# Two spikes buffers in turn, one transposed input, bias rows by TensorE, stages laid anew

## The reference

```
xn = layernorm(x)                        # x: 4 x 4096 x 512
s  = attn(xn);  g = silu(ffn(xn));  return x + s * g

attn: xs = rmsnorm(xn[:, ::2]) * g_norm;  xp, gate = split(xs @ w_in.T + b_in)
      for each of 2048 steps:  h = tanh(h * A + xt[:, :, None] * Bm)    # 4 x 512 x 64
                               y = h @ Cm.sum(0) + Dv * xt
      out = repeat((y * silu(gate)) @ w_out.T + b_out, 2)
ffn:  spikes = sigmoid(xn @ W_enc + b_enc)                              # 1024 wide
      cont = spikes @ W_s2c + b_s2c                                     # 64 wide
      gate = top 2 of softmax(cont @ Wr + br), 8 experts
      eo = sum_e gate_e * (relu(cont @ W1_e + b1_e) @ W2_e + b2_e)
      layernorm(sigmoid(eo @ W_c2s + b_c2s) @ W_dec + b_dec) * ln_g + ln_b
```

## Time and profile before

| | us |
|---|---|
| median of 3 runs (5712.73 to 5716.41) | 5715.25 |
| the profiled execution | 5713.89 |
| its span | 5712.1 |
| PE busy | 5333.2 (93%) |
| DVE busy | 5449.9 (95%) |
| POOL busy | 5221.4 (91%) |
| ACT busy | 4504.0 (79%) |

### The profile page before, as it was taken

How to read it: one execution, slowest core, us unless ns; L and a number is a source line. 1 busy time by engine, 2 the same in 40 slices (tenths; PEclk the granted TensorE clock), 3 DMA queues, 4 the chain that set the end, 5 groups by cost and what they waited for, 6 DMA issues and landing times.

```text
span 5712.1 us, 92986 instructions
## 1 busy us (share of the span) xinstructions
PE 5333.2 (93%) x30820; PEld 2810.7 (49%) x30820; DVE 5449.9 (95%) x9300; ACT 4504.0 (79%) x9558; POOL 5221.4 (91%) x2764
## 2 busy tenths in 40 slices
PE   6999999999999999999999999999999999999998
PEld 3545545545455455454454554544545545445453
DVE  5999999999999999999999999999999999999998
ACT  5778778787787787877877878778778787787786
POOL 4999999999999999999999999999999999999997
PEclk9999999999999999999999999999999999999999
DMA  6454454444544545444445454444444544444443
GB/s 163 115 122 113 118 122 111 122 113 119 121 113 119 123 109 124 113 118 122 114 118 123 109 125 113 119 121 114 119 123 107 125 114 118 122 114 119 122 108 92
DMA packets 158294, 673.71 MB, mean 118 GB/s; under 512 B 45780, under 2 KB 46840, under 8 KB 92280
## 3 DMA queue, kind: packets, MB, share of 16 engines
q1 hardware_dynamic: 157816, 667.76, 48.5%
HBM read 617.26 MB, written 50.33 MB: 117 GB/s over the span
## 4 chain that ended last, share of the span: by engine, by line
PE 75%; ACT 11%; DVE 8%; issue 4%; SPq 1%; DMA 0%; POOLq 0%; POOL 0%; ACTq 0%; DVEq 0%
PE bank L868 15%; PE ps_y L837 12%; PE bank L927 10%; PE bank L856 8%; PE bank L989 8%; PE ps_acc L989 8%; ACT hidden L676 7%; PE ps_acc L944 4%; DVE ps_z L1109 4%; DVE ps_z L1103 2%; PE bank L910 2%; PE ps_acc L955 2%; PE bank L972 1%; PE ps_acc L972 1%; ACT h L563 1%
## 5 line engine op out<-in xcount | busy, mean ns | idle before, releaser
L497 POOL TENSOR_TENSOR u<-xb,bt 128x1024 f32<-128x1024 f32 x2048 | 4822.6, 2361 | 421.3 <-DVE ps_z L1109 358.3
L563 ACT ACTIVATE h<-ps_z 128x512 f32<-128x512 f32 x4096 | 2419.9, 600 | 839.5 <-DVE ps_z L1109 795.1
L1103 DVE TENSOR_TENSOR ps_z<-h,ps_A 128x512 f32<-128x512 f32 x4096 | 2674.9, 691 | 188.0 <-ACT h L563 106.9
L1109 DVE TENSOR_TENSOR ps_z<-ps_z,u 128x512 f32<-128x512 f32 x4096 | 2660.2, 691 | 0.0
L837 PE MATMUL ps_y<-h,c_wide 128*32 128x512 f32 x8192 | 973.1, 598 | 0.0
L868 PE MATMUL bank<-xnT,w_enc 128*128 128x256 f32 x4096 | 911.9, 381 | 2.0 <-ACT wide L629 2.0
L676 ACT ACTIVATE hidden<-bank,bias_cols 128x256 f32<-128x256 f32 x2048 | 808.0, 475 | 128.5 <-PE bank L927 118.3
L868 PEld LDWEIGHTS bank<-xnT,w_enc 128*128 128x128 f32 x4096 | 772.9, 190 | 185.4 <-issue 83.4
L927 PE MATMUL bank<-contT_both,w 64*128 64x256 f32 x4096 | 582.9, 400 | 198.6 <-ACT hidden L676 105.2
L927 PEld LDWEIGHTS bank<-contT_both,w 64*128 64x128 f32 x4096 | 381.9, 186 | 462.4 <-ACT hidden L676 205.0
L944 PE MATMUL ps_acc<-hidden,w 128*64 128x256 f32 x4096 | 540.3, 389 | 28.9 <-DVE wide L1157 24.2
(11 more groups left out here) (122 smaller groups left out, 3751.4 us busy)
## 6 DMA issues: line engine op xcount, KB each, us to landing
xb<-x_proj_scratch SPq DMA_DIRECT2D x2048, 256.0 KB, 4.6
xbuf<-in_L_attn_x SPq DMA_DIRECT2D x256, 128.0 KB
xres<-in_L_attn_x SPq DMA_DIRECT2D x512, 64.0 KB
out<-g SPq DMA_DIRECT2D x256, 128.0 KB
x_proj_scratch<-xp SPq DMA_DIRECT2D x256, 64.0 KB
w_in<-in_L_attn_w_in SPq DMA_DIRECT2D x1, 2048.0 KB, 8.1
w_enc<-in_L_ffn_W_enc SPq DMA_DIRECT2D x1, 2048.0 KB
w_dec<-in_L_ffn_W_dec SPq DMA_DIRECT2D x1, 2048.0 KB
```

The lines of the kernel that those rows point to most:

```text
L497: pool.tensor_tensor(u[:, tau % 2, :, :], xt, bt[:, :, :], ALU.mult).then_inc(u_ready, 1)
L563: act.activation(h[:, tau % RING, f, :], ps_z[:, f, :], ACT.Tanh).then_inc(h_ready, 1)
L1103: dve.tensor_tensor(ps_z[:, f, :], h[:, (tau - 1) % RING, f, :], ps_A[:, f, :], ALU.mult).then_inc(m_done, 1)
L1109: dve.tensor_tensor(ps_z[:, f, :], ps_z[:, f, :], u[:, tau % 2, f, :], ALU.add).then_inc(z_ready, 1)
```

## The change

Four things. `wide` gets two buffers, by the block's parity, and `xnT` has one instead of two. The bias rows b_dec and b_out are no longer copied by ACT: they lie in one tile `bias_three` with ln_b, and PE adds a row by a matmul with a column of the identity, as it already did for ln_b. So `dec_seed` and `out_seed` are gone, and `decode` (twice) and `fin_out` begin with a `bias_row`. And the table of slots is new throughout.

```diff
-        xnT = sb("xnT", [P, 2, KD, 2, P])
+        xnT = sb("xnT", [P, KD, 2, P])
-        wide = sb("wide", [P, KH, T2])
+        wide = sb("wide", [P, 2, KH, T2])
...
-PE_UP = (19.75, 24.6875, 26.5625, 30.8125, 32.4375, 33.1875, 33.625, 35)
-PE_DOWN = (23.5, 26.5625, 29.3125, 32.75, 33.5, 34.625, 35.5625, 36.5)
+PE_UP = (12.75, 14, 16.0625, 18, 18.75, 20.8125, 22.5, 24.5625)
+PE_DOWN = (14.25, 15.1875, 18.4375, 18.5625, 22.4375, 24.375, 26.9375, 29.0625)
...
-            def dec_seed(blk, q):
-
-                if q == 0:
-                    wait_free(act, "DEC", blk)
-                else:
-                    act.wait_ge(acc_drained, 2 * blk + 1)
-                act.activation(dec_out[q][:, :], b_dec_all[:, :], ACT.Copy).then_inc(dec_seeded, 1)
...
-            def out_seed(blk):
...
-                act.activation(bank[1][:, :], b_out_all[:, :], ACT.Copy).then_inc(out_seeded, 1)
...
+            def bias_row(dst, row, start, stop):
+                return pe.matmul(dst[:, :], ident[:, row:row + 1].to_broadcast([P, P]), bias_three[:, :],
+                                 start=start, stop=stop, skip_group_check=True)
+
+            def decode(blk, par, q):
+                if is_first(blk) and q == 0:
+                    pe.wait_ge(biases_shifted, 2)
+                if q == 0:
+                    wait_free(pe, "DEC", blk)
+                else:
+                    pe.wait_ge(acc_drained, 2 * blk + 1)
                 dst = dec_out[q]
+                bias_row(dst, ROW_DEC, True, False)
                 for k in range(KH):
...
             def fin_out(blk):
                 wait_drained(pe, "FIN", blk)
-                pe.wait_ge(out_seeded, blk + 1)
+                wait_free(pe, "OUT", blk)
+                bias_row(bank[1], ROW_OUT, True, False)
                 for k in range(KD):
```

More of the change, by code:

```diff
@@ L71 @@
[L71 to L83, removed]
@@ new lines @@
+SP_RESIDUAL = (28.375, 44.875)
+SP_STORE_OUT = 61.625
+POOL_PROJ_SCALE = -23.5
+POOL_DEC_SCALE = (38.6875, 39.25)
+POOL_FIN_SKIP = 4.625
+POOL_FIN_ADD = (42.8125, 51.125)
+ACT_PROJ_NORM = -23.4375
+ACT_PROJ_EVAC = (-23, -19.125)
+ACT_PROJ_SEED = (-21.125, -10.125)
+ACT_PROJ_OUT = (-19.5, -8.125)
+ACT_Y_SEED = 5.75
+ACT_SPIKES = (-6.5, -6.3125, -1.375, -0.4375)
+ACT_SPIKES_FIRST = (4.6875, 3.25, 5.375, 8.75)
+ACT_CONTT_COPY = 9.5
+ACT_ROUTE_SIG = 12.9375
+ACT_DUP_COPY = 9.8125
+ACT_G_COPY = (14.9375, 14.9375)
@@ L292, in build @@
                  + [("C2S1", PE_TO_SPIKES[0]), ("DEC", PE_DECODE[0]), ("OUT", PE_FIN_OUT)]]
+        FIRST_FILLS = {f"ENC{n}": PE_ENCODE_FIRST[n] for n in range(4)}
         bank_of = {name: side for side in range(2) for name, _ in FILLS[side]}
@@ L295, in build @@
         for side in range(2):
-            order = sorted((STEPS * blk + slot, blk, k) for k, (_, slot) in enumerate(FILLS[side]) for blk in range(NB))
+            order = sorted((STEPS * blk + (FIRST_FILLS.get(name, slot) if blk == 0 else slot), blk, k)
+                           for k, (name, slot) in enumerate(FILLS[side]) for blk in range(NB))
             for n, (_, blk, k) in enumerate(order):
@@ L855, in proj_in @@
                 for k in range(KD):
-                    ins = pe.matmul(bank[half][:, :], xnT[:, par, k, 0, :], w_in[:, k, D * half:D * half + D],
+                    ins = pe.matmul(bank[half][:, :], xnT[:, k, 0, :], w_in[:, k, D * half:D * half + D],
                                     start=False, stop=(k == KD - 1), skip_group_check=True)
@@ L868, in encode, with encode_first, controller @@
                         ins = pe.matmul(bank[n % 2][:, T2 * half:T2 * half + T2], w_enc[:, k, P * m:P * m + P],
-                                        xnT[:, par, k, :, :], start=(k == 0 and half == 0), stop=(k == KD - 1),
+                                        xnT[:, k, :, :], start=(k == 0 and half == 0), stop=(k == KD - 1),
                                         skip_group_check=True)
                 filled(ins, ENC[n])
-            def controller(blk):
+            def encode_first(blk, par, n):
+                encode(blk, par, n)
+            def controller(blk, par):
                 pe.wait_ge(acc_seeded, blk + 1)
@@ L879, in controller @@
                         wait_drained(pe, ENC[k // 2], blk)
-                    ins = pe.matmul(contT_acc[M * half:M * half + M, :], w_s2c[:, k, :], wide[:, k, :],
+                    ins = pe.matmul(contT_acc[M * half:M * half + M, :], w_s2c[:, k, :], wide[:, par, k, :],
                                     start=False, stop=(k >= KH - 2), skip_group_check=True)
@@ L1043, in _ @@
             ins.then_inc(columns_summed, 1)
+            proj_in(0, 0, 1)
             def between(blk, par, slot):
@@ L1055, in between @@
                 for n in range(4):
-                    if slot == PE_ENCODE[n]:
+                    if slot == PE_ENCODE[n] and not is_first(blk):
                         encode(blk, par, n)
+                    if slot == PE_ENCODE_FIRST[n] and is_first(blk):
+                        encode_first(blk, par, n)
                 if slot == PE_CONTROLLER:
-                    controller(blk)
+                    controller(blk, par)
                 if slot == PE_ROUTER:
```

165 lines of the change are left out of this document (76 added, 89 removed).

## The result

| | before | changed |
|---|---|---|
| median, us | 5715.28 (4 runs, 5712.73 to 5716.41) | 5798.26 (4 runs, 5796.79 to 5799.76) |
| ratio, 95% interval | | 1.0147 [1.0135, 1.0159] |
| span of the profiled execution | 5712.1 | 5795.7 |

The account below looks back on a forecast made before the run. It took a block as PE's work plus PE's waits, with PE and DVE both nearly full. 5713.89 + 76 (blocks) + 17 (end) = 5807 us, given as 5806; range 5755 to 5858, the likeliest case's own 5773 to 5860.

Parts of the forecast that it names:

- PE's work: Three bias-row matmuls a block on PE at 0.883 us each: +2.65 us a block, between 2.58 and 2.91.
- PE's waits: PE's idle time in a block: 3.45 us instead of 4.87, in the rounds, second `up`, `dup` and third `up`.
- The third wait of 0.7: One of three PE waits for relus in rounds without a `y` between, 0.7 us each.
- the four waits that were to go: PE's waits behind `fin_mul` (1.0), at the second transpose (0.9), between `fold` and `to_spikes` (0.5), behind `gate_pair` (0.4).
- the 0.4 behind `gate_pair`: PE's wait at `down` behind `gate_pair`, 0.4 us a block, said to be gone in the new order.
- its 2.1: PE's waits in the rounds of `up` and `down`: three of 0.7 us, together 2.1 us a block.
- The block: Block length: +2.65 - 1.42 = +1.23, taken as +1.2 us, about 89.0; sixty-three blocks make +76 us.
- DVE's waits: DVE's waits for late tanhs: longer than 1.6 us a block, most of them in steps 16 to 21.
- The end: After the last tanh: `fin_mul` starts 26 to 29 us later instead of 8.9; +17 us, about 39 instead of 22.
- the floor: Lower limit of a block: some 86.2 us, 87.80 less all of DVE's 1.6 us of waits.
- the faster rival: ACT's relief leaves PE only 0.5 to 1.5 us of waits a block: 5630 to 5686 us, say 5680; chance 0.14.
- ACT's load is not the lever: Removing ACT's three bias copies, 0.60 to 0.63 us each, was costed at nothing; PE idles for single instructions' turnaround.

Follow-up runs that it names:

- e1: Changed kernel without its three bias rows a block, so b_dec and b_out are not added; 5785.65 us, ratio 1.0124, block 88.58 us.
- e10: Kernel before, in its own order, without ACT's three bias copies and without rows in their place; 5704.23 us, ratio 0.9979, block 87.66 us.
- e3: Changed kernel with the fifth `up` ahead of the fourth `down` on TensorE; 5798.31 us, ratio 1.0141.
- The halves: Changed kernel, fourth and fifth steps' readouts cut in halves laid into TensorE's relu waits, fourth `down` behind fifth `up`; 5774.64 us, ratio 1.0104.
- e12: Changed kernel with the halves and, in the last block alone, the first decode ahead of the last readout on TensorE; 5765.61 us, ratio 1.0087.

## Why the prediction was right, and where it was not

- **PE's work.** Forecast +2.65 us, measured +2.25. The rows themselves are 0.96, 0.86 and 0.86 us from start to start (2560.93 to 2561.89, 2568.76 to 2569.62, 2580.72 to 2581.58), as taken. What the term left out: the groups that now stand behind a row became shorter. Groups by form of the changed kernel give 592 ns for the decoder into its first bank and for the output:

```profile
L986 PE MATMUL bank<-w_dec,wide 128*128 128x512 f32 x1024 | 449.9, 592 | 0.0
L1011 PE MATMUL bank<-w_out,oT 128*128 128x512 f32 x512 | 230.2, 592 | 0.0
```

  Before they were 605 ns and took 466.0 and 236.8 us, so 22.7 us over 64 blocks, 0.35 a block, came back. For the output it need not be a bias row: in e1 its matmuls take 592 ns too, and there they stand directly behind the ln bias row.
- **PE's waits.** Forecast 3.45 us, measured 3.54, mostly at the places named: 0.70 at the fourth `down` and 0.70 at the eighth `up`, the second `up` 0.9 for `xnT` (0.75 said), `dup` 0.5. The third wait of 0.7 is split: 0.32 at the seventh `up`, and 0.34 at the `down` ahead of it for a gate product of DVE. So of the four waits that were to go three went, and the 0.4 behind `gate_pair` is still there as these 0.34. The sum is near all the same, since the forecast had that time inside its 2.1 as well.
- **The block.** Forecast +1.2, measured +0.92; the difference is mostly the smaller work (0.40), against 0.09 more of waits.
- **DVE's waits** are longer than 1.6, as said, three of the five in steps 16 to 21, with 1.7 of the 2.2 us.
- **The end.** `fin_mul` starts 27.8 us after the last tanh (26 to 29 said), and the end is at 40.9 us instead of 39. It grew by 18.9 where 17 was taken; some 2.3 us of it is the slow stretch below, which the forecast did not have.
- **Not foreseen: the first block**, 6.6 us longer. It has places of its own for `encode`. DVE waits once for 4.95 us there, since the tanh stands on ACT behind an eviction that waits 4.0 us for PE's `encode`, and that `encode` had itself waited 7.9 us for ACT to empty the banks. DVE's and then ACT's rows:

```profile
89.90 0.70 DVE L1103 TENSOR_TENSOR ps_z<-h,ps_A 128x512 f32<-128x512 f32 x1 [4.95 <-ACT h L562]
```
```profile
ACT wide L628 <- PE bank L852: 4.0, 1, 4.0
```

  Forecast were 76 us for the blocks and 17 for the end, 93; measured 64.7 ahead of the last tanh's end and 18.9 behind it, 83.6. Part of that nearness is luck: the other blocks gave 18 us less than forecast, and the first block and the end gave 8.5 back.
- **A slip in the sum.** The profiled execution lies 1.4 us below the median, so 5807 should have gone up to 5808 and not down to 5806. It decides nothing here.

**The frame of the sum held for the kernel as it ran, not for what lies around it.** "The length of a block is PE's work plus PE's waits" is an account that closes for any kernel; as a cause it holds in the old order (waits of 4.75 to 4.89 whatever the work) and above 88.58 us in the new one (3.54 and 3.56). The weak step is the floor: "it can't fall below some 86.2". No run went below it, but it was taken from DVE with all of its waits gone, and it is far too low for the new order. Those waits come from the rounds, where ACT has more to do than a step is long, and from a ring of `up`, relus and `down`. In e1, with b_dec and b_out off PE, DVE's 32 steps of 2.56 us make 81.9, its other work in steps 5 to 12 (counted from 0) adds 3.3, and in steps 14 to 25, those of the rounds, gate products and waits for `h` add another 3.3: 88.6. So the price of the faster rival, 5630 to 5686 us, was out of reach of what was taken off PE here: without rows the kernel took 5785.65, and with the late rounds filled as well 5761.84. And "the change costs the rows, less the waits that close" reads as if taking the rows back would give the time back. It gives 12.6 us of 83.6.

That ACT's load is not the lever was right. By the Trainium skill, page "Perfetto Trace Analysis", section "Optimization Strategies", the engines to speed up when the matmul engine idles are those that block the critical path. ACT is such an engine by name in PE's waits, but with the copies gone in the order of before its work fell from 70.18 to 68.87 us a block and the block by 0.14 only. PE waits for the turnaround of single instructions, not for ACT's total, and the copies were none of these.

What stays open: which of the moves in the new order makes up the 0.92 us that it costs without rows. The places are known from the steps: over 2.56 us each, steps 14 to 25 hold 3.34 us in e1 and 2.15 in e10, and all others 0.25 less in e1. Step 18 alone has 1.31 against 0.28, but when one move took its wait away (e3), the next step had it. The stretch from the second to the eighth `up` is 20.61 us in e1 and 19.45 in e10, and the first `down` (about 1.0) now stands inside it, where it stood ahead of the second `up` before. That makes this move a candidate; no run put it back. The halves take back 0.38 of the 0.92, without undoing any move.

## What to carry to other kernels

Work moved from an engine with time to spare to one that sets the pace was paid in full here in the old order, and the new order had a price of its own: run both halves apart, since the sum alone (here +0.92 us a block) hides one of +2.43 and one of +0.92 that overlap. Where two cycles are nearly level, taking work off one of them gains only the distance to the other, while shortening a stretch that both share gains on both; a floor for the second must keep those of its waits that come from its own queue. In-order engines make couples: when one instruction is moved to a later place, move with it what stands behind its result on every other engine, or a wait as long as the move appears there.

## What was not expected of the hardware

TensorE's clock fell in the tail. Windows of the changed kernel's end (columns as above, the clock is the third value from the end):

```profile
5747.20:5754.80 7.60, 0.37 (x4) 0.00 (x0) 6.80 (x12) 4.24 (x9) 4.02 (x2) 0.86 0.00 0
5754.80:5760.00 5.20, 5.19 (x19) 1.46 (x20) 0.69 (x1) 1.42 (x4) 0.00 (x0) 0.54 0.01 3
5760.00:5775.00 15.00, 15.00 (x40) 6.82 (x39) 0.76 (x1) 0.99 (x3) 0.74 (x2) 1.00 0.00 0
```

PE idles 7.25 us for the last tanh and then works at a granted clock of 0.54, nearly all of it at the lower level, 1.2 GHz, before it is back at 1.00:

```profile
5754.81 3.64 PE L821 MATMUL ps_y<-h,c_wide 128*32 128x512 f32 x16 [7.25 <-ACT h L562]
5758.39 1.69 PE L967 MATMUL bank<-bias_three,ident 128*128 128x512 f32 x2
5759.91 7.03 PE L986 MATMUL bank<-w_dec,wide 128*128 128x512 f32 x16
```

The readout and the row take 5.10 us from the first start to the decode's; the same pair at full clock takes 2.81 in run e12 (from 5735.89 to the decode at 5738.70), so the clock cost some 2.3 us here. In that run PE worked in the gap and the clock was 1.00 in this stretch:

```profile
5727.00:5736.00 9.00, 8.30 (x22) 3.37 (x26) 6.27 (x11) 5.04 (x12) 3.50 (x2) 1.00 0.01 2
```

The Trainium skill, page "TensorE: Matmul & The Clock Gate", section "What's actually happening", says that idling brings the clock down to 1.2 GHz and work brings it back to 2.4; these rows agree.
